# Sixteen-head cross-attention pair on one core: one PSUM bank for the loop's helper items, three banks for score rows, value matmuls in groups of four

## The reference

```
x = layernorm(x + attn(x, x, x, causal))                  # layer 0, self-attention
x = layernorm(x + attn(x, ctx, ctx))                      # layer 0, cross-attention, 1500 keys
x = layernorm(x + moe(x))                                 # 8 experts, top 2
q, c = rmsnorm(x) * g_q, rmsnorm(ctx) * g_c               # layer 1
s = (q @ Wq) (c @ Wk)^T / sqrt(8), masked; a = softmax(s)
x = rmsnorm(x + (a @ (c @ Wv)) @ Wo) * g_out
```

## Time and profile before

| | us |
|---|---|
| median of 3 runs (634.06 to 639.16) | 634.29 |
| the profiled execution's own time | 629.88 |
| its span, first to last instruction | 628.0 |
| loop of layer 0, about | 92 to 311 |
| loop of layer 1, about | 403 to 621 |

### The profile page before, as it was taken

The page is one execution under the profiler, slowest core; times in us unless marked ns, Lnnn a source line. Parts: engine busy times, 40 slices in busy tenths (PEclk is TensorE's granted clock), DMA queues, the critical chain, the costliest instruction groups (busy, mean ns, idle before and its releaser), DMA issues.

```text
span 628.0 us, 17882 instructions
## 1 busy us (share of the span) xinstructions
PE 547.8 (87%) x6536; PEld 386.4 (62%) x6536; DVE 425.5 (68%) x814; ACT 366.2 (58%) x718; POOL 213.7 (34%) x361
## 2 busy tenths in 40 slices
PE   6978669999999999999879993799989988998995
PEld 4765436766766676666647773457656665766763
DVE  1789867785776778687353215887869786876753
ACT  2445328675775866667524432476656766675663
POOL 6485232030321226272123002444626353521011
PEclk9677659998999999999959996799999998998898
DMA  5426558646366383636502220356353642528000
GB/s 157 89 76 192 190 144 215 202 151 178 125 163 179 104 215 125 176 112 172 150 0 67 67 68 15 115 178 183 127 167 122 169 148 74 152 70 222 2 3 16
DMA packets 41101, 79.77 MB, mean 127 GB/s; under 512 B 9326, under 2 KB 19246, under 8 KB 41054
## 3 DMA queue, kind: packets, MB, share of 16 engines
q1 hardware_dynamic: 41054, 79.16, 43.1%
HBM read 58.95 MB, written 20.13 MB: 126 GB/s over the span
## 4 chain that ended last, share of the span: by engine, by line
PE 68%; DVE 10%; SPq 6%; issue 5%; POOL 4%; ACT 4%; DMA 3%; ACTq 0%; POOLq 0%; DVEq 0%
PE bank L395 14%; PE bank L429 13%; PE bank L407 11%; PE bank L357 6%; PE bank L363 6%; PE bank L1265 5%; PE bank L1254 4%; DVE mx L591 3%; PE bank L351 3%; DVE key_ss L624 1%; DMA k_scratch<-kparts 1%; PE bank L369 1%; PE bank L374 1%; ACT kparts L510 1%; POOL scratch L1622 1%
## 5 line engine op out<-in xcount | busy, mean ns | idle before, releaser
L591 DVE TENSOR_REDUCE mx<-bank 112x1 f32<-112x500 f32 x384 | 250.1, 674 | 63.7 <-PE bank L395 59.3
L544 ACT ACTIVATE scratch<-bank 125x448 f32<-125x448 f32 x384 | 203.9, 548 | 128.2 <-PE bank L407 125.8
L395 PE MATMUL bank<-krep,qfix 96*112 96x500 bf16 (+1 forms) x384 | 157.9, 421 | 16.9 <-DVE mx L591 9.2
L407 PEld LDWEIGHTS bank<-qfix,krep 99*128 99x128 bf16 (+1 forms) x1536 | 112.2, 101 | 51.6 <-issue 21.5
L407 PE MATMUL bank<-qfix,krep 99*128 99x112 bf16 (+1 forms) x1536 | 139.4, 215 | 0.0
L429 PE MATMUL bank<-scratch,v 125*32 125x112 f32 x3072 | 114.9, 266 | 5.3 <-ACT scratch L544 4.1
L395 PEld LDWEIGHTS bank<-krep,qfix 96*112 96x112 bf16 (+1 forms) x384 | 51.2, 135 | 54.7 <-issue 32.3
L429 PEld LDWEIGHTS bank<-scratch,v 125*32 125x32 f32 x3072 | 67.4, 109 | 25.0 <-ACT scratch L544 7.2
L718 POOL TENSOR_TENSOR oT<-comb,rec 128x56 f32 (+1 forms) x32 | 9.9, 310 | 163.0 <-DVE rec L613 163.0
L707 POOL TENSOR_TENSOR kparts<-k_rest,kparts 128x500 bf16<-128x500 f32 x48 | 54.5, 1136 | 29.6 <-ACT kparts L528 29.5
L1265 PEld LDWEIGHTS bank<-scratch 128*112 128x112 f32 x256 | 33.1, 183 | 15.7 <-issue 10.4
(11 more groups left out here) (170 smaller groups left out, 734.3 us busy)
## 6 DMA issues: line engine op xcount, KB each, us to landing
krep<-k_scratch SPq DMA_DIRECT2D x192, 187.5 KB, 3.8
k_scratch<-kparts SPq DMA_DIRECT2D x16, 1125.0 KB, 4.6
ctx_tile<-in_ctx SPq DMA_DIRECT2D x16, 750.0 KB
scratch<-in_L_xattn_e_w SPq DMA_DIRECT2D x16, 256.0 KB, 3.1
Q<-q_scratch SPq DMA_DIRECT2D x12, 168.0 KB, 3.2
q_scratch<-scratch SPq DMA_DIRECT2D x6, 168.0 KB, 2.4
Q<-q_scratch SPq DMA_DIRECT2D x12, 56.0 KB, 2.2
k_rest<-in_selq SPq DMA_DIRECT2D x1, 576.0 KB, 9.5
```

The source lines that it names most:

```text
L395: nc.tensor.matmul(row_bank(v, c, lead)[0:PQ, 0:KB], qfix[0:KR[l], slot, p * PQ:(p + 1) * PQ], krep[0:KR[l], slot, p, n * KB:(n + 1) * KB] ...
L407: ins = nc.tensor.matmul(SCORES[c % 3][:, p * PQ:(p + 1) * PQ], krep[0:KS[l], slot, p, c * KP:c * KP + 128], qfix[0:KS[l], slot, p * PQ:(p ...
L544: nc.scalar.activation(P[:, p_slot(s_, slot), :], SCORES[slot % 3][0:KP, 0:UQ], ACT.Exp, scale=SCALE).then_inc(z["exp_ok"], 1)
L591: nc.vector.tensor_reduce(mx[:, par, c // NKB, c % NKB:c % NKB + 1], row_bank(v, c, lead)[0:PQ, 0:KB], AX.X, ALU.max).then_inc(z["row_max" ...
```

## The change

Seven edits go together.

1. Items in the loop use bank 6 alone (index 0), and each waits until the item just before it was taken.
2. Transposed scores keep three banks (3, 4, 7), and rows have three (1, 2, 0): a loop row waits for the maximum of the row three before it. The rows ahead of the loop go around five banks in another order (`LEAD_BANKS`).
3. `pe_st` waits for the exponential three before it also in slots 0 to 2, in steps 1 to 3 (its argument `slot` is the step's copy of the keys).
4. Value chunks go in groups of four: in slots 5 and 9 and in slot 1 of the next step (behind the last slot in step 3), instead of pairs in 3, 5, 7, 9, 11 and 1.
5. SP's `sp_qparts(0, 0)` stands ahead of the key write of batch 1.
6. In the prologue DVE's `dve_qparts` follows batch 7 instead of 6, ACT's `act_first_odd` the whole loop over batches; PE does the outputs of the last batch before the first queries.
7. POOL's mask work moves to batch 6 and one reciprocal deviation behind the last key part.

```diff
-        ROWS, SCORES, OUT, MISC = bank[0:2], bank[2:5], bank[5], bank[6:8]
+        ROWS, SCORES, OUT, MISC = (bank[1], bank[2], bank[0]), (bank[3], bank[4], bank[7]), bank[5], bank[6:8]
+        LEAD_BANKS = (SCORES[0], SCORES[1], ROWS[1], ROWS[2], ROWS[0])
...
-            return ([*ROWS, *SCORES])[(12 * v + c + 1) % 5] if lead else ROWS[c % 2]
+            return LEAD_BANKS[(12 * v + c + 4) % 5] if lead else ROWS[c % 3]
...
-                pe.wait_ge(z["row_max"], 12 * v + c - 1)
+                pe.wait_ge(z["row_max"], 12 * v + c - 2)
...
-            if c >= 3:
+            if c >= 3 or slot > 0:
                 pe.wait_ge(z["exp_ok"], 12 * u + c - 2)
...
-                before = [("V", 2 * j, 2, 0, l), ("D", 4 * j - 1, 0, 3, l)]
+                before = [("D", 4 * j - 1, 0, 3, l)]
                 order_ = before + full_order(l, j)
...
-                            pe_item(pe, item, k, order_[k])
+                            pe_item(pe, item, 0, order_[k])
                             k += 1
                         pe_st(pe, l, u, s_, slot)
                         if slot == 1 and s_ > 0:
-                            pe_pv_two(pe, l, j, s_ - 1, 10)
-                        if slot >= 3 and slot % 2:
-                            pe_pv_two(pe, l, j, s_, slot - 3)
+                            pe_pv_four(pe, l, j, s_ - 1, 8)
+                        if slot in (5, 9):
+                            pe_pv_four(pe, l, j, s_, slot - 5)
                     if s_ == 3:
-                        pe_pv_two(pe, l, j, s_, 10)
+                        pe_pv_four(pe, l, j, s_, 8)
...
             sp_ctx(sp, 0, 3, 1)
+            sp_qparts(sp, 0, 0)
             sp_kwrite(sp, 0, 1, 1)
...
+            outputs(B - 1)
             pe.wait_ge(L[0]["v_ok"], 2)
             pe_first_queries(pe, 0)
-            outputs(B - 1)
...
-                if b == 6:
-                    act_first_odd(act, 0)
+            act_first_odd(act, 0)
             act_first_fixed(act, 0)
...
-                if b == 6:
+                if b == 7:
                     dve_qparts(dve, link, 0)
```

More of the change, by code:

```diff
@@ L431, in pe_pv, with pe_pv_four @@
             ins.then_inc(z["pv_ok"], 1)
-        def pe_pv_two(pe, l, j, s_, first):
-            for c in range(first, first + 2):
+        def pe_pv_four(pe, l, j, s_, first):
+            for c in range(first, first + 4):
                 pe_pv(pe, l, j, s_, c)
@@ L547, in body @@
                             if item[0] != "D":
-                                act_item(act, item, k)
+                                act_item(act, item, 0)
                             k += 1
@@ L660, in body @@
                             if item[0] in "KD":
-                                late.setdefault(slot + 1, []).append((*item, k))
+                                late.setdefault(slot + 1, []).append((*item, 0))
                             k += 1
@@ L678, in body @@
                         dve_comb(dve, l, u)
-                        dve_recip(dve, l, u, k)
+                        dve_recip(dve, l, u, 0)
                         k += 1
@@ L1114, in _ @@
             sp_prepare(sp)
-            sp_qparts(sp, 0, 0)
             sp.wait_ge(s["mask_ok"], 1)
@@ L1642, in _ @@
                     key_ones({1: 0, 3: 1, 4: 2, 5: 3}[b], b + 3)
-                if b in (4, 7):
-                    self_rstd({4: 0, 7: 1}[b])
+                if b == 4:
+                    self_rstd(0)
                 if b == 2:
@@ L1654, in _ @@
                         pool_low(pool, 0, *PROLOGUE[k][1:4])
-            pool.wait_ge(s["in_mask"], 32)
-            nc.gpsimd.tensor_copy(mask_col[:, :, :], mask_col8[:, :, :]).then_inc(s["identb_ok"], 1)
-            nc.gpsimd.tensor_scalar(mask_row, mask_row8[:, :], BIG, -BIG, ALU.mult, ALU.add).then_inc(s["mask_ok"], 1)
+                if b == 6:
+                    pool.wait_ge(s["in_mask"], 32)
+                    nc.gpsimd.tensor_copy(mask_col[:, :, :], mask_col8[:, :, :]).then_inc(s["identb_ok"], 1)
+                    nc.gpsimd.tensor_scalar(mask_row, mask_row8[:, :], BIG, -BIG, ALU.mult, ALU.add)\
+                        .then_inc(s["mask_ok"], 1)
+                if b == 7:
+                    self_rstd(1)
             self_rstd(TT - 2)
```

## The result

The changed kernel takes 766.86 us (median of 4 runs, 762.25 to 767.91), and the kernel before takes 636.66 us beside it. The ratio is 1.203 (95% interval 1.195 to 1.211): slower, 14 us above the forecast of 753 and inside the range. The profiled execution took 767.91 us with a span of 766.1.

What follows compares the result with a forecast made beforehand. PE was taken to bound the loops. From 629.9 us: item waits +122, groups of four -24, third row bank -10, prologue -2.5, clock +33 gave 748, plus 4.4 for the median: 753 us, own range 735 to 775 (chance 0.53).

Steps and rivals of the forecast that it cites:

- The bound: In the two loops PE sets the time (busy 51.90 of 55.40 us); its waits are added whole.
- The item waits: Single item bank in the loops: each item waits for the one before; 17.2 us per full iteration, 122 us in all.
- K behind D: Slot 6 of step 2: K waits for D's reciprocal, 0.7 us more, 0.62 being there already.
- the scores behind the M copy: Step borders: next step's scores wait for ACT's M copy, net 0.6 us at three borders, 1.8 an iteration.
- The clock: Loops: item waits make PE's granted clock fall, costing about 33 us, bounds 0 and 77.
- The rival in which the clock holds: Loops: same item waits but no clock falls, 720 us; chance 0.20 for 700 to 735.
- The rival at half the time down: Loops: clock down half the time, 797 us; chance 0.20, shared with no saving by groups.
- The third row bank: Loop rows: PE no longer waits behind the key squares, 8 x 1.2 = 10 us gained, bounds 0 and 14.
- The groups of four: Value chunks in the loops: 88 fewer groups at 0.27 us each, 24 us gained.
- nothing takes this back: Groups' 24 us saving stays whole, since no chunk waits for an exponential in the rows but at the iteration's end.
- The prologue: Before the loop: earlier query DMAs and a later split remove waits, 2.5 us gained, between 7.7 gained and 2 lost.
- The sum: Whole kernel: 629.9 + 122 - 24 - 10 - 2.5 + 33 = 748 us, median 4.4 above, so 753.

Runs made afterwards that it cites:

- the fillers: Kernel with one item bank and two row banks (780.87 us), plus unread matmuls into the free bank just ahead of items that wait: 741.73 us, ratio 1.173.
- the run with the mask ahead: Kernel before with the changed prologue and the mask's write to DRAM ahead of the query parts on SP, nothing else: 624.59 us, ratio 0.987.

## Why the prediction was right, and where it was off

*The bound.* PE sets the time in the loops, and what makes it wait is added whole: shown by the run with one bank alone (119 us from one edit that adds no work). The last iteration, which has hardly any items, did not become longer.

*The item waits.* Right in kind at every place named: T 0.96 (up to 2.24 in layer 1, where up to 1.4 stood before), K 1.35, D 1.76, K behind D 1.19, V 1.72 as the profile counts them, against 1.12, 1.5, 1.9, 1.3 (0.7 on top of the 0.62 that was there) and 1.9; V waited 15 times for 24.5 us, where 15 times 1.9 was forecast. Right in size too: PE's list of waits has 102 us at the items and at the scores behind the M copy, against 6 in the kernel before, and the brackets hide 0.15 to 0.2 at each of some 100, so the waits added are about 110 to 115 us (an estimate), where 122 were forecast. The clock in the loops, forecast near 0.85, was 0.80 to 0.86. A full iteration, forecast at 68 to 75 us, took 70.6 to 79.7, six of the seven above 75, and PE was busy 78 to 81% of it, where well under 80% was forecast.

*The clock.* 33 forecast, at least 39 measured by the fillers. The rival in which the clock holds (720) fell with that, and with it the rule of the Trainium skill ("TensorE: Matmul & The Clock Gate", section "Why this matters for your kernels") as a bound for this kernel: no wait inside an iteration was as long as the gap that the rule names (the longest in the list is 2.2 us), and in the three iterations read window by window the clock fell three or four times in each. The rival at half the time down (797) was too high.

*The third row bank.* 10 forecast with bounds 0 and 14; 14 measured (up to 21 by the ratios). The place was right in the main, the key squares of layer 1, but the mechanism only in part: the row waits 0.6 to 0.8 there, not 1.2, and the rest is the clock that falls behind the wait. Rows wait for DVE elsewhere too, which groups of four bring about; that this gains nothing once it is removed, since V then waits longer, is shown by layer 0.

*The groups of four.* This is the step that failed: 24 us gained, and "nothing takes this back". The saving of starts was right in size for PE's own time: a group of four takes 0.91 to the next row, as forecast (0.90). But alone it gave a loss of some 4 to 5, and in the changed kernel a loss of 19 to 23. Chunk pairs were PE's cover for DVE and ACT. The prediction used that where it charged V, T and the M copy for missing chunks, but it did not ask it of the rows, nor whether idle PE time brings clock falls with it. It thus priced the groups partly as a gain and partly, under other names, as a cost, and so the sum came out nearer than this one term.

*The prologue.* A gain of 2.5 forecast, between a gain of 7.7 and a loss of 2; nothing measured. The reason named as a danger (the mask write late) took the place of the waits removed, and the run with the mask ahead shows what all three together were worth: 8.8.

*The sum.* At the clock of before, the change would be some 728 us (741.7 with fillers and two row banks, less 14 for the third; an estimate, since the 14 were measured without fillers and hold some clock), where the prediction without its clock term had 720; the clock gives 6 of the 14 us that were missing. Of the other 8, the prologue has some 2; with 21 for the third bank the rest would be gone. The kernel before differs by 5.7 us from set to set (631.0 to 636.7), so that it stays open how these last us divide.

## What to carry to other kernels

A second PSUM bank for small helper products can be worth much (here 119 us of 631), because PE, which takes its work in order, stops with everything behind an item that waits for another engine to take the last one; if a bank must be given up, the item whose consumer comes late in its engine's order should not share the one that is left (here D: 70 us). Work that looks badly batched may be the cover of a chain elsewhere: before grouping it, ask what each piece lies between. And where several waits end at one place, read when each of them ends: here moving two of three gave nothing, and moving all three 8.8 us.

## What was not expected of the hardware

Matmuls that nobody reads made the kernel faster: 780.87 to 741.73 us with groups of four, 750.05 to 727.24 with pairs, because PE kept its upper clock level (mean 0.851 to 0.927, and 0.884 to 0.920). Waits of 1 to 2 us often brought the level down, though not each time, and the next item then ran at half speed with PE busy throughout, as at 274.20 above.
